# Selective scan of a fused decoder: the sums over the states done for two units at once, over three areas of states

## The reference

```
xn = layernorm(x);  xi, z = split(xn @ W_in)            # 256 inner channels each
u  = silu(causal depthwise conv of xi, 4 taps)
dt, Bm, Cm = split(u @ W_xproj)                         # 8, 64 states, 64 states
delta = softplus(dt @ W_dt + b_dt);  A = -exp(A_log)    # A: [256, 64]
for t in range(128):
    h = h * exp(delta[t] * A) + (delta[t] * u[t]) * Bm[t]    # h: [batch, 256, 64]
    y[t] = sum over the 64 states of h * Cm[t]
out = x + ((y + u * D) * silu(z)) @ W_out
```

## Time and profile before

| | us |
|---|---|
| median of 3 runs | 1403.27 (1398.83 to 1403.92) |
| the profiled execution, its own time | 1392.82 |
| its span, first to last instruction | 1390.8 |
| scan block, about | 75.7 to 429.4 |
| block of `mamba_output`, about | 429.9 to 444.1 |

### The profile page before, as it was taken

One profiled execution on the slowest core, in us unless ns is written; L12 is line 12 of the kernel. 1 busy time (PEld: TensorE's weight loads), 2 busy tenths in 40 slices (PEclk: granted clock), 3 DMA queues, 4 the chain that ended last, 5 costly groups with the idle time before them and its releaser, 6 DMA issues. The chain is left out here.

```text
span 1390.8 us, 29830 instructions
## 1 busy us (share of the span) xinstructions
PE 1114.5 (80%) x12054; PEld 800.1 (58%) x12065; DVE 850.9 (61%) x1500; ACT 529.5 (38%) x1322; POOL 570.0 (41%) x382
## 2 busy tenths in 40 slices
PE   5568898898887898999547598689476899866895
PEld 2158787887875454545336255545366454543695
DVE  6577888888884476366713476567512676755233
ACT  2433434434431363255114164156133565612121
POOL 4169988989864702210157310020434201000432
PEclk9656988888878599999869799699688998987998
DMA  2099687778855200000075100000365000000793
GB/s 105 0 207 216 196 214 206 203 208 211 204 168 198 65 1 1 0 1 2 1 201 182 33 2 1 1 1 1 116 199 185 1 2 1 1 1 23 259 302 99
DMA packets 74232, 139.75 MB, mean 100 GB/s; under 512 B 8129, under 2 KB 28369, under 8 KB 73745
## 3 DMA queue, kind: packets, MB, share of 16 engines
q1 hardware_dynamic: 70128, 129.67, 32.8%
q0 software_dynamic: 3968, 8.18, 1.6%
HBM read 128.06 MB, written 14.82 MB: 103 GB/s over the span
## 5 line engine op out<-in xcount | busy, mean ns | idle before, releaser
L658 ACT ACTIVATE shifted_a<-scores,nmax_a 128x128 f32<-128x128 f32 x768 | 208.5, 387 | 85.7 <-DVE nmax_a L624 85.7
L1125 PE MATMUL decay<-delta,A_pairs 32*128 32x127 f32 x2048 | 178.6, 335 | 49.2 <-DVE small_pack L1219 18.9
L1200 ACT ACTIVATE decay<-decay 128x1016 f32<-128x1016 f32 x128 | 128.7, 1010 | 197.8 <-PE decay L1125 197.8
L1125 PEld LDWEIGHTS decay<-delta,A_pairs 32*128 32x128 f32 x2048 | 155.5, 235 | 69.6 <-DVE small_pack L1219 23.6
L624 DVE TENSOR_REDUCE nmax_a<-scores 128x4 f32<-128x512 f32 x192 | 123.6, 686 | 108.3 <-PE scores L563 105.9
L361 POOL TENSOR_TENSOR rstd<-ve,neghalf 128x4 f32<-128x4 f32 x30 | 31.5, 1051 | 281.7 <-DVE ve L347 281.7
L630 DVE COPY PTs_a<-PT 128x512 f32<-128x512 f32 x192 | 123.6, 681 | 4.6 <-PE PT L571 4.6
L571 PE MATMUL PT<-mamba_pack,shifted_a 128*128 128x128 f32 x768 | 114.1, 293 | 4.3 <-DVE PTs_a L630 2.7
L1460 POOL DMA_INDIRECT results<-xs_s x76 | 73.0, 960 | 104.2 <-DVE xs_s L1632 96.6
L571 PEld LDWEIGHTS PT<-mamba_pack,shifted_a 128*128 128x128 f32 x768 | 88.5, 149 | 36.8 <-issue 20.1
L247 PE MATMUL norm_ps<-identb 128*128 128x512 bf16 x180 | 59.6, 446 | 52.2 <-DVE ve L347 51.5
(11 more groups left out here) (395 smaller groups left out, 2238.3 us busy)
## 6 DMA issues: line engine op xcount, KB each, us to landing
pos_bias<-du_rows SPq DMA_DIRECT2D x72, 256.0 KB, 4.9
small_pack<-L3f_w SPq DMA_DIRECT2D x15, 768.0 KB, 5.0
XN<-du_rows SPq DMA_DIRECT2D x38, 256.0 KB, 5.1
XNT<-du_rows SPq DMA_DIRECT2D x38, 256.0 KB, 4.8
O<-du_rows SPq DMA_DIRECT2D x36, 256.0 KB, 4.9
masked_cos<-du_rows SPq DMA_DIRECT2D x36, 256.0 KB, 4.9
masked_sin<-du_rows SPq DMA_DIRECT2D x36, 256.0 KB, 4.8
small_pack<-L2f_w SPq DMA_DIRECT2D x15, 514.0 KB, 5.0
```

Of the source, the lines that this page charges most:

```text
L658: t = nc.scalar.activation(shifted[u % 4][:, j, :], scores[u % 4][:, j, :], ACT.Exp, scale=-1.0, bias=nmax[:, u % 4, j:j + 1])
L1125: t = nc.tensor.matmul(decay[k % DEEP][:, s, i, 1:S], A_pairs[strip, c, 4 * q + i, :, :].rearrange("p j n -> p (j n)"), delta[strip, c, b ...
L1200: nc.scalar.activation(x, x, ACT.Exp).then_inc(decayed, 1)
```

## The change

The sums of both units of a batch are made together. One product per token has 128 moving columns (the 64 pairs of both units) in place of two products of 64 columns. That needs the states of two units at once while a third is written, so there are three areas in one tensor `space` of 96 KB per partition. To make room, the tensors that only later stages use (`small_pack`, `row_pack`, `rel`, `q_mask`, `k_mask`, the masks in bf16, `run_on`) are allocated behind the scan, and everything that fills them moves from `start_stage` and from the end of the scan into the block of `mamba_output`. `B2` and `C2` use the buffers of `CT` and `CTOK`, so these two loads move as well. `mask8` is still loaded at the start.

The loop of PE has slots of a batch: `slot = (k - 18) % 16`. Slots 0 to 6 have the sums of the batch whose last tile was scanned (16 or 20 products each, 128 in all), slot 9 has `turn_back` for both units (16 products), and slots 12 to 15 have four filler products each, of 128 rows by 128 weight columns by 256 moving columns in bf16, into a part of `YT` that nothing reads. By this condition (`slot > PARTS + 4`) four of the nine slots without sums have fillers. `k` = 0 and 1 have them too (their slots are 14 and 15).

```diff
 # scan_block
-    UNITS, PER, DEEP = B * IC, 8, 3
+    UNITS, PER, DEEP, PARTS = B * IC, 8, 3, 7
+    BOTH = IC * PER
-        h = [m.small_pack[:, 0:S * PAIRS], sb("h1", [128, S * PAIRS])[:]]
+        area = lambda n: n % 3 * AREA
+        def at_token(b, token):
+            first = space[:, area(IC * b) + token:area(IC * b) + token + 1]
+            return bass.AP(first.tensor, first.offset,
+                           [first.ap[0], [area(IC * b + 1) - area(IC * b), IC], [S, PAIRS]])
...
-            sp.wait_ge(summed, UNITS - 1)
-            sp.dma_start(m.small_pack[:], m.dram["small"]).then_inc(m.loaded_small, 16)
...
+            def gather(b, part):
                 if part == 0:
-                    pe.wait_ge(scanned, (n + 1) * PER)
+                    pe.wait_ge(scanned, (b + 1) * BOTH)
...
+                for turn in range(32 * part // PARTS, 32 * (part + 1) // PARTS):
+                    half = turn // 16
                     for i in range(4):
+                        token = 64 * half + 16 * i + turn % 16
+                        t = nc.tensor.matmul(Y[32 * i:32 * i + 32, b % 2, half, :, :], Cz[:, token, :],
+                                             at_token(b, token), start=(turn % 16 == 0), stop=(turn % 16 == 15))
...
-            for k in range(TILES + 18):
+            for k in range(TILES + 12):
                 if k < TILES:
                     multiply(k)
-                if k >= 11 and (k - 11) % 8 < 4 and (k - 11) // 8 < UNITS:
-                    gather((k - 11) // 8, (k - 11) % 8)
-                if k >= 17 and (k - 17) % 8 == 0 and (k - 17) // 8 < UNITS:
-                    turn_back((k - 17) // 8)
+                b, slot = (k - BOTH - 2) // BOTH, (k - BOTH - 2) % BOTH
+                if 0 <= b and slot < PARTS:
+                    gather(b, slot)
+                if 0 <= b and slot == PARTS + 2:
+                    turn_back(b)
+                if k < TILES and slot > PARTS + 4:
+                    if b >= 0:
+                        pe.wait_ge(y_copied, b + 1)
+                    for _ in range(4):
+                        nc.tensor.matmul(YT[:, 2:4, :], m.identb[:], bcast_mid(m.identb[:], 2), start=True, stop=True)
 # scan_block, DVE
-                if n >= 2 and k % PER == 0:
-                    dve.wait_ge(summed, n - 1)
+                if n >= 3 and k % PER == 0:
+                    dve.wait_ge(summed, (n - 3) // IC + 1)
 # start_stage, SP
-            sp.dma_start(m.row_pack[:], d["rows"].to_broadcast([128, ROWS_N])).then_inc(m.loaded_rest, 16)
-            sp.dma_start(m.CT[:], d["ctx_feat"]).then_inc(m.loaded_rest, 16)
-            sp.dma_start(m.CTOK[:], d["ctx_tok"]).then_inc(m.loaded_rest, 16)
-            sp.dma_start(m.rel[:], d["rel_pos"]).then_inc(m.loaded_rest, 16)
 # EarlyWork (in mamba_output), SP
+            sp.wait_ge(m.loaded_rest, 16)
+            sp.dma_start(m.rel[:], m.dram["rel_pos"]).then_inc(m.loaded_rest, 16)
+            first = SMALL_AT["L0f_router"][0]
+            sp.dma_start(m.small_pack[:, 0:first], m.dram["small"][:, 0:first]).then_inc(m.loaded_small, 16)
+            sp.dma_start(m.CT[:], m.dram["ctx_feat"]).then_inc(m.loaded_late, 16)
+            sp.dma_start(m.row_pack[:], m.dram["rows"].to_broadcast([128, ROWS_N])).then_inc(m.loaded_late, 16)
+            sp.dma_start(m.CTOK[:], m.dram["ctx_tok"]).then_inc(m.loaded_late, 16)
+            sp.dma_start(m.small_pack[:, first:], m.dram["small"][:, first:]).then_inc(m.loaded_late, 16)
             sp.wait_ge(copied, 1)
             sp.dma_start(tab, tableT[:]).then_inc(stored, 16)
             sp.wait_ge(stored, 16)
...
+            sp.wait_ge(m.loaded_late, 64)
```

More of the change, by code:

```diff
@@ L137 @@
 ROWS_AT, ROWS_N = layout(ROWS)
+AREA = 8 * B * S
 class Model:
@@ L148, in sb, with sb_above @@
             return ctx.enter_context(nc.sbuf_tensor(name, shape, dt))
+        def sb_above(name, shape, dt=F32):
+            return ctx.enter_context(nc.sbuf_tensor(name, shape, dt, side="right"))
         def sem(name):
@@ L745, in emit @@
                                                              "table_stored"))
-        widened = m.sem("mask_widened")
+        widened, masks_set = m.sem("mask_widened"), m.sem("masks_set")
         tab = m.dram["rel_table"]
@@ L1145, in gather, with turn_back @@
+                if part == PARTS - 1:
                     t.then_inc(summed, 1)
-            def turn_back(n):
-                b, c = n // IC, n % IC
-                pe.wait_ge(sum_copied, n + 1)
-                if n >= 2:
-                    pe.wait_ge(y_copied, n - 1)
-                for j in range(2):
-                    rows = slice(64 * j, 64 * j + 64)
-                    for half in range(2):
-                        at = slice(64 * half, 64 * half + 64)
-                        nc.tensor.matmul(YT[rows, n % 2, at], D_order[:, c, rows],
-                                         u[:, c, b * S + 64 * half:b * S + 64 * half + 64], start=True, stop=False)
-                        t = nc.tensor.matmul(YT[rows, n % 2, at], Ys[n % 2][:, half, :],
-                                             m.w("alternate")[:, rows], start=False, stop=True)
+            def turn_back(b):
+                pe.wait_ge(sum_copied, b + 1)
+                if b >= 1:
+                    pe.wait_ge(y_copied, b)
+                for c in range(IC):
+                    for j in range(2):
+                        rows = slice(64 * j, 64 * j + 64)
+                        for half in range(2):
+                            at = slice(64 * half, 64 * half + 64)
+                            nc.tensor.matmul(YT[rows, c, at], D_order[:, c, rows],
+                                             u[:, c, b * S + 64 * half:b * S + 64 * half + 64], start=True, stop=False)
+                            t = nc.tensor.matmul(YT[rows, c, at], Ys[:, half, c, :], m.w("alternate")[:, rows],
+                                                 start=False, stop=True)
@@ L1173, in place_c @@
                 if b:
-                    act.wait_ge(summed, IC * b)
+                    act.wait_ge(summed, b)
                 for j in range(2):
@@ L1200, in _ @@
                     nc.scalar.activation(x, x, ACT.Exp).then_inc(decayed, 1)
-                if k % 16 == 8 and 0 < k // 16 < B:
-                    place_c(k // 16)
-                if k >= 15 and (k - 15) % 8 == 0 and (k - 15) // 8 < UNITS:
-                    copy_sum((k - 15) // 8)
-                if k >= 18 and (k - 18) % 8 == 0 and (k - 18) // 8 < UNITS:
-                    copy_y((k - 18) // 8)
+                b, slot = (k - BOTH - 2) // BOTH, (k - BOTH - 2) % BOTH
+                if b >= 0:
+                    if slot == PARTS:
+                        copy_sum(b)
+                    if slot == PARTS + 1 and b + 1 < B:
+                        place_c(b + 1)
+                    if slot == PARTS + 3:
+                        copy_y(b)
         @block.vector
@@ L1213, in _ @@
                 n = k // PER
-                out = h[n % 2][:, k % PER * T:(k % PER + 1) * T]
+                out = space[:, area(n) + k % PER * T:area(n) + (k % PER + 1) * T]
                 dve.wait_ge(decayed, k + 1)
                 dve.wait_ge(fed, k + 1)
-                if n >= 2 and k % PER == 0:
-                    dve.wait_ge(summed, n - 1)
+                if n == 2 and k % PER == 0:
+                    for stored in du_stored:
+                        dve.wait_ge(stored, 16 * IC)
+                if n >= 3 and k % PER == 0:
+                    dve.wait_ge(summed, (n - 3) // IC + 1)
                 nc.vector.tensor_tensor_scan(out, decay[k % DEEP][:].rearrange("p s i t -> p (s i t)"),
```

104 lines of the change are left out of this document (51 added, 53 removed).

## The result

The changed kernel takes 1429.05 us (median of 4 runs, 1427.99 to 1435.08) against 1401.05 us for the kernel before on the same chip (4 runs, 1398.79 to 1403.92): ratio 1.0183, 95% interval 1.0145 to 1.0222 (the two medians alone give 1.020). It is slower, and outside the range of the prediction.

The account below looks back on a forecast made before the run. It took POOL's pace as the scan's floor, with PE costing some 3.9 us per batch. Terms -6.0 - 11.9 - 1.3 + 9.1 + 2.0 = -8.1 us gave 1384.7 profiled, 1395.2 from the median; range 1377 to 1412.

Parts of the forecast that it names:

- about 27 ns per record at either clock ... I take 27 and 53 ns: PE's sums: 64-column records 27 ns; 128-column records 27 ns at 2.4 GHz, 53 at 1.2; saves 6.9 us per batch at full clock.
- The floor of 37.3 us a batch: Scan: POOL's pace, two tiles in 4.69 us, taken as 2.33 us per tile, limits a batch of 16.
- the fillers, put at 1.5 us a batch: Slots 12 to 15: filler products show as 1.5 us late per batch; bounds a gain and 2.9 us lost.
- The first 16 tiles: Start of the scan, no sums due for 18 tiles: 44.0 us before, 38.0 after, saves 6.0.
- the block: `mamba_output`: 6.5 MB of loads lose their cover, 23.3 us against 14.2, cost 9.1 us (bounds 7 and 12).
- the products at 1.2 GHz: Stage after `mamba_output`: PE stands some 6 us, then starts 3.67 us of 512-column products at 1.2 GHz, +2 us (0 to 4).
- the pauses that go: End of the scan: PE's "issue" pauses shrink with no load beside them, -2.5 us of a net -1.3.
- DVE's wait for `summed`: Slot 6: DVE waits for sums reading the area it writes next, about 0.3 us added per batch.
- some 3 us into its sums: Scan: each batch loses the full clock around slots 9 to 12 and regains it then (bounds 1 and 6.7 us).
- rival B: Scan: clock returns only three slots into the sums, batch 42 us, scan saves 0.5 in all, 1412.6 us; chance 0.20.
- The 81 ns: PE's sums: 81 ns per weight load and matmul, 20.7 us per batch instead of 6.9, some 1505 us; chance 0.01.
- my chance for slower, 0.19: Whole kernel: chance of a slower result, given as rival B with the worst of the loads.

Follow-up runs that it names:

- the even kernel with two fillers: Kernel before, a unit's sums spread over 7 slots instead of 4, two filler products ahead of `multiply` in the slot without sums: 1371.02 us, ratio 0.9867; repeated 1380.43 us.
- the run with the loads alone: Kernel before with only the loads moved into the block of `mamba_output`, scan as before: 1409.45 us, ratio 1.003.
- adjacent reads: Changed kernel with the sums' moving columns at step 1 within each area, so reading other states than they should: 1409.29 us, ratio 1.002.

## Why the prediction was wrong

**The step that failed** is "about 27 ns per record at either clock ... I take 27 and 53 ns" for 128 columns. It joined rows of two different reads: the sums of the earlier trace rows have strided columns, 64 of them, and the attention's rows have 128 adjacent ones. Each row was read rightly; the columns' distance, which no row shows but the code does, decides. A strided column costs 0.4 ns at either clock, so 256 records of 128 cost what 512 of 64 did: 13.6 against 13.8 us, saving nothing. In seven slots instead of eight they are then packed more densely, 3.2 us on the mean (1.09 + 1.86 or 2.29) instead of 2.25. Put into the forecast's own sum, with 5.5 slots of a batch at the full clock, as it had them: 39.5 + 5.5 x 0.95 = 44.7 a batch, measured 44.5; 6.94 batches 310.2, measured 310.3; the tail's 185 records at the full clock 26 ns dearer, -1.3 + 4.8 = +3.5, measured +3.5. The total would have been +32.8 and 1436 from the median; 1429 came.

That the batch comes out to 0.2 us is in part luck, for two other terms were off in opposite directions. The floor of 37.3 us a batch, by POOL's 4.69 us for two tiles, was too high: the even kernel with two fillers ran whole batches in 36.1 (18.05 a unit), with POOL busy throughout. And the fillers, put at 1.5 us a batch with 2.9 as the bound, cost about 3 (experiment without them).

**The other steps.** The first 16 tiles (-6.0, measured -7.2, by the floor that was too high), the block (+9.1, measured +8.0, ended by SP behind the store, as forecast) and the products at 1.2 GHz (+2.0, measured +2.9) were right, and so were the pauses that go (-2.5; the run with the loads alone shows -4.2 in the tail). The start was put at 0, and the 2.3 us there are of the kind that comes and goes between runs. The filler slot, 3.05 forecast, took 2.97 us. DVE's wait for `summed` was put at 0.3 and took 2.46: it follows from the slow sums, since the last part ended later, and with adjacent reads it is 0.3 at most.

**The clock.** Its return "some 3 us into its sums" holds for the changed kernel (2.1 to 3.0 us in six batches, 8.2 in the first). It doesn't for the fast reads for which it was meant, where it took two to four slots; had the 27 ns been right, rival B would have come out, not the forecast. The 81 ns by which the Trainium skill (page TensorE: Matmul & The Clock Gate, section Back-to-back issue gap) would have it slower was rightly set aside: a record took 26 ns with adjacent columns and 53 to 55 with strided ones. The sign was that of the rule, by another mechanism, and my chance for slower, 0.19, rested on the clock and the loads alone; that the reads might cost by the column was not among the rivals.

## What to carry to other kernels

Before two rows are joined into a price, compare the access patterns in the code, not only the shapes in the profile: a product's columns may be bound by the reading of its moving operand, as here with fp32 columns 128 elements apart, and then merging two products saves nothing. And where TensorE's clock changes within a loop, spread its work evenly and test a filler or two in the slot that lacks work: the same sums took 51.3 us a batch without and 36.1 with them. But time it: in the kernel before fillers brought nothing, and in the changed one they cost. Price a stage by several executions; here one profile of before was 14 us faster than the next.

## What the runs showed of the hardware

- The moving operand of an fp32 product (here with 32 weight columns) reads columns 2 elements apart at 28.8 ns per record of 128, nearly the full rate (26.4), and from 4 elements on at half of it, 53 to 54 ns, up to 57.6 at 32. This cost doesn't change with TensorE's clock (96 columns at step 128: 38.3 ns at 2.4 GHz, 38.9 at 1.2). Steps of 3 elements and other types were not tried.
- Busy isn't enough for the clock: 282 us busy of 282 at 0.50 without fillers, 203.3 of 203.8 at 1.00 with 0.6 us of 128-row, 128-column bf16 products in each unit of 18. Which property of the products counts (rows, columns, type) was not tried apart.
- The loss can be long: from about one pause of 0.53 us on the clock stayed at 0.50 for 65 us. That the pause caused it was seen once and not tested, and what ends such a stretch stays open.
